# Reordering the start, the output add and the scale loads of a fused retention and mixture-of-experts kernel on one core

## What is computed

```python
# block 1: chunked retention, 8 heads of 16, chunks of 64 tokens
x = x + retention(layernorm(x), Wq, Wk, Wv) @ Wo
#   attn  = (q k^T) * D              inside a chunk, D a decay table
#   o     = attn v + (q * decay_q) S
#   S_new = decay_s * S + (k * decay_k)^T v
# block 2: 8 experts, each token takes the best 2
x = x + ffn(layernorm(x))
#   probs = softmax(n @ Wg);  top 2, weights divided by their sum
#   h = square(relu(n @ W1[e]));  y = h @ W2[e];  out = sum_e combine[e] * y
```

## Time and profile before

| | us |
|---|---|
| three runs | 320.14, 324.41, 324.46 (median 324.41) |
| the profiled execution: its own time | 321.02 |
| its span, first to last instruction | 319.2 |
| PE busy in the span | 285.7 (90%) |
| DVE, POOL, ACT busy | 216.2, 205.5, 180.4 |
| mean granted TensorE clock, of full speed | 0.957 |

### The profile page before, as it was taken

The page is one execution under the profiler, slowest core; times in us unless marked ns, Lnnn a source line. Parts: engine busy times, 40 slices in busy tenths (PEclk is TensorE's granted clock), DMA queues, the critical chain, the costliest instruction groups (busy, mean ns, idle before and its releaser), DMA issues.

```text
span 319.2 us, 8925 instructions
## 1 busy us (share of the span) xinstructions
PE 285.7 (90%) x3662; PEld 224.8 (70%) x3662; DVE 216.2 (68%) x561; ACT 180.4 (57%) x258; POOL 205.5 (64%) x166
## 2 busy tenths in 40 slices
PE   7968838898899889998999879998999889989995
PEld 5655537576688667875888658876888668868883
DVE  2853805788176965599476945599476927998873
ACT  2451633555387465756476545756476545767772
POOL 2134628968366885777985794777985767466553
PEclk9996995799799999999999998999999999999999
DMA  7345009007001261033402180000700070016000
GB/s 244 104 132 169 2 23 310 3 2 239 30 1 35 70 206 61 0 101 104 166 3 65 37 258 10 0 35 24 247 1 36 6 264 1 25 47 227 3 33 33
DMA packets 13577, 26.80 MB, mean 84 GB/s; under 512 B 1120, under 2 KB 6624, under 8 KB 13536
## 3 DMA queue, kind: packets, MB, share of 16 engines
q1 hardware_dynamic: 13536, 26.23, 25.1%
HBM read 24.00 MB, written 2.23 MB: 82 GB/s over the span
## 4 chain that ended last, share of the span: by engine, by line
PE 64%; DVE 16%; issue 12%; POOL 5%; ACT 2%; POOLq 1%; DVEq 0%
PE h_ps L323 8%; PE h_ps L325 7%; PE h_ps L324 7%; PE y_ps L338 6%; PE y_ps L344 5%; PE y_ps L339 5%; POOL act_lo L1061 5%; PE bank L471 3%; PE bank L483 3%; DVE attn L650 3%; PE bank L496 3%; DVE act_s L759 2%; DVE out_sb L780 2%; PE bank L404 2%; DVE combine_r L749 2%
## 5 line engine op out<-in xcount | busy, mean ns | idle before, releaser
L1061 POOL TENSOR_TENSOR act_lo<-act_f,act_hi 128x512 fp32r<-128x512 f32 x112 | 146.8, 1332 | 68.4 <-ACT act_f L946 68.3
L759 DVE SCALAR_TENSOR_TENSOR act_s<-h_ps,scale 128x1024 f32<-128x1024 f32 x64 | 78.1, 1220 | 61.2 <-PE h_ps L325 58.2
L941 ACT ACTIVATE act_hi<-act_s 128x1024 fp32r<-128x1024 f32 x64 | 68.0, 1063 | 58.8 <-DVE act_s L759 58.7
L946 ACT ACTIVATE act_f<-act_s 128x1024 f32<-128x1024 f32 x64 | 66.9, 1046 | 0.0
L323 PE MATMUL h_ps<-x_hi,w_lo 128*128 128x512 f32 x128 | 54.4, 425 | 3.2 <-ACT o_t L912 3.2
L338 PE MATMUL y_ps<-act_hi,w_lo 128*128 128x512 f32 x128 | 54.8, 428 | 2.0 <-issue 2.0
L325 PE MATMUL h_ps<-x_hi,w_hi 128*128 128x512 f32 x128 | 51.7, 404 | 0.0
L324 PE MATMUL h_ps<-x_lo,w_hi 128*128 128x512 f32 x128 | 51.7, 404 | 0.0
L339 PE MATMUL y_ps<-act_hi,w_hi 128*128 128x512 f32 x128 | 51.6, 403 | 0.0
L344 PE MATMUL y_ps<-act_lo,w_hi 128*128 128x512 f32 x128 | 41.2, 403 | 0.1
L323 PEld LDWEIGHTS h_ps<-x_hi,w_lo 128*128 128x128 f32 x128 | 24.9, 195 | 8.8 <-ACT o_t L912 3.4
(11 more groups left out here) (135 smaller groups left out, 413.3 us busy)
## 6 DMA issues: line engine op xcount, KB each, us to landing
scale<-scratch SPq DMA_DIRECT2D x32, 512.0 KB, 6.0
x_t_in<-x_tr SPq DMA_DIRECT2D x8, 256.0 KB, 4.2
x_all<-x SPq DMA_DIRECT2D x8, 256.0 KB, 4.2
out<-out_sb SPq DMA_DIRECT2D x8, 256.0 KB, 2.1
scale<-w SPq DMA_DIRECT2D x1, 768.0 KB, 4.8
cst<-constants SPq DMA_DIRECT2D x1, 417.0 KB, 5.3
cst<-constants SPq DMA_DIRECT2D x1, 256.0 KB, 2.8
scale<-w SPq DMA_DIRECT2D x1, 256.0 KB, 6.1
```

What stands on the lines that cost most here:

```text
L759: nc.vector.scalar_tensor_tensor(out=act_s[:, u % 2], in0=h_ps[:, u % 2], scalar=0.0, in1=scale[:, f % 2, e].unsqueeze(1).to_broadcast([P, ...
L941: nc.scalar.activation(act_hi[:, u % 4], act_s[:, u % 2], ACT.Square).then_inc(act_hi_ready, 1)
L946: nc.scalar.activation(act_f[:, u % 2], act_s[:, u % 2], ACT.Square).then_inc(act_f_ready, 1)
L1061: nc.gpsimd.tensor_tensor(act_lo[:, u % 4, n], act_f[:, u % 2, n], act_hi[:, u % 4, n].bitcast(F32), ALU.subtract).then_inc(pool_low_ready, 1)
```

## The change

Six edits, all of them in the order of work:

- **Start.** On TensorE the products of tile 1 go further forward, the W1 pieces behind them, and `transpose_roots(0)` stands ahead of `w1_product(0, 0)`; ScalarE's and GpSimd's orders follow.
- **Router.** `route` uses `x_sum` and `wg_whole` in float32, 4 products in place of 8, and doesn't wait for `x_lo`. `shift_logits` reads the logits from PSUM without a sum first.
- **`low_x`** goes from GpSimd, ahead of `low(u + 1)`, to VectorE, behind `scale_h(f, 6)`.
- **Small products.** `outputs_within` is cut into halves in slots 13 and 14, `outputs_before` goes from slot 14 to slot 15. `transpose_roots` goes from slot 11 to slot 12.
- **VectorE.** `spread_roots` stands behind the second `decay_scores` product of four, and its sum becomes a `tensor_reduce`. `add_experts(f - 1)` goes from behind `scale_h(f, 3)` to behind `scale_h(f, 7)`.
- **Quarters.** The four quarters of `scale` get waits that spread them in time.

```diff
             def scales(s):
...
                 for j in range(PARTS):
-                    if s >= 2:
-                        sp.wait_ge(act_s_ready, EXPERTS * (s - 2) + PER_PART * (j + 1))
+                    if j == 0 and s >= 2:
+                        sp.wait_ge(act_s_ready, EXPERTS * (s - 1))
+                    if j == 1 and 1 <= s and s + 1 < TILES:
+                        sp.wait_ge(av_done, s + 2)
+                    if j >= 2:
+                        sp.wait_ge(act_s_ready, EXPERTS * s + 2 * j - 3)
...
             def route(s):
-                r = s % X2T_RING
-                pe.wait_ge(x_hi_ready, s + 1)
-                pe.wait_ge(x_lo_ready, s + 1)
                 pe.wait_ge(x_sum_ready, s + 1)
+                pe.wait_ge(x_hi_ready, s + 1)
...
-                for g in range(GROUPS):
-                    o = bank1[:, 2 * EXPERTS * g:2 * EXPERTS * (g + 1)]
-                    pe.matmul(o, x_lo[:, r, P * g:P * (g + 1)], parts, start=True, stop=False)
-                    last = pe.matmul(o, x_hi[:, r, P * g:P * (g + 1)], parts, start=False, stop=True)
+                for g in range(GROUPS):
+                    last = pe.matmul(bank1[:, EXPERTS * g:EXPERTS * (g + 1)], x_sum[:, s % SUM_RING, P * g:P * (g + 1)],
+                                     wg_whole[:], start=True, stop=True)
...
-                    if n == 11:
+                    if n == 12:
                         transpose_roots(p)
...
                     if n == 13:
-                        outputs_within(a)
+                        outputs_within(a, (0, 1))
                     if n == 14:
+                        outputs_within(a, (2, 3))
+                    if n == 15:
                         outputs_before(a)
...
-                nc.vector.tensor_tensor(combine_r[:].rearrange("p e g -> p g e"), spread[:, :, 0], spread[:, :, 1],
-                                        ALU.add).then_inc(combine_ready, 1)
+                nc.vector.tensor_reduce(combine_r[:], spread[:].rearrange("p g k e -> p e g k"), AX_X, ALU.add
+                                        ).then_inc(combine_ready, 1)
...
                 scale_h(f, 3)
                 low(u + 2)
-                if f >= 1:
-                    add_experts(f - 1)
                 if p < TILES:
                     choose(p)
...
                 if a < TILES:
-                    decay_scores(a, decay_order(a)[1:])
+                    decay_scores(a, decay_order(a)[1:2])
                 if p < TILES:
                     spread_roots(p)
+                if a < TILES:
+                    decay_scores(a, decay_order(a)[2:])
                 scale_h(f, 5)
...
                 scale_h(f, 6)
                 low(u + 5)
+                if p < TILES:
+                    low_x(p)
                 if a + 1 < TILES:
                     statistics(a + 1, 0)
                 scale_h(f, 7)
                 low(u + 6)
+                if f >= 1:
+                    add_experts(f - 1)
```

More of the change, by code:

```diff
@@ L460, in state_updates, with outputs_within @@
                 last.then_inc(u_done, 1)
-            def outputs_within(s):
+            def outputs_within(s, groups):
                 b = s % 2
-                pe.wait_ge(attn_ready, PAIRS * (s + 1))
-                pe.wait_ge(update_ready, 2 * (s + 1))
-                for g in range(GROUPS):
+                if groups[0] == 0:
+                    pe.wait_ge(attn_ready, PAIRS * (s + 1))
+                    pe.wait_ge(update_ready, 2 * (s + 1))
+                for g in groups:
                     for j in range(2):
@@ L565, in _ @@
             project_qk(1)
-            outputs_within(0)
+            outputs_within(0, (0, 1, 2, 3))
+            project_v(1)
             outputs_before(0)
+            transpose_k(1)
+            project_out(0)
+            scores(1)
+            transpose_x2(0)
             center_piece(1)
-            project_out(0)
-            project_v(1)
-            transpose_k(1)
-            transpose_x2(0)
-            scores(1)
             route(0)
+            project_qk(2)
             center_piece(2)
-            project_qk(2)
+            transpose_k(2)
             center_piece(3)
-            transpose_k(2)
             center_piece(4)
+            transpose_roots(0)
+            w1_product(0, 0)
+            state_updates(1)
             project_v(2)
-            state_updates(1)
-            w1_product(0, 0)
-            outputs_within(1)
+            outputs_within(1, (0, 1, 2, 3))
             outputs_before(1)
-            transpose_roots(0)
             w1_product(0, 1)
@@ L1088, in _ @@
                     root_variance(p, 1)
-                    low_x(p)
                 low(u + 1)
```

112 lines of the change are left out of this document (51 added, 61 removed).

## The result

The changed kernel takes **330.94 us** in the median of four runs (329.40 to 335.95), the kernel before in the same comparison 323.80 (320.14 to 324.46). The ratio is 1.022, with a 95% interval from 1.013 to 1.031: it is slower, though whether by more than 2% stays open. The forecast was 323, near no change, with a range of 307 to 335: the time lies in the range, but the kernel got slower where no change was forecast. The profiled execution took 329.40, its span 327.6, at a mean granted clock of 0.951.

The account below looks back on a forecast made before the run. The prediction took TensorE, busy for 90% of the span, and its idle gaps as the bound. From the profiled execution: 321.0 - 11 - 7.3 - 7.7 - 3.0 + 26.3 + 5.0 = 323.3 us, forecast 323, range 307 to 335.

Parts of the forecast that it names:

- the start: Ahead of the first W2 product: the new order wins 11 us, between 8 and 13; under 8 refutes the prediction.
- The output add and SyncE's order: Tile boundaries: the store waits for the late add, delaying scratch write and quarters; 26.3 us plus 5.0 of half clock.
- The root wait: At `transpose_roots` in the loop: the wait for `combine_r` goes, a gain of 7.3 of 8.25 us.
- Issue stalls: TensorE's four issue gaps in the loop go because quarters start later: 7.7 us, plus 3.0 for clock dips.
- The third rival: Loop: issue stalls stay since bursts of small products cause them, not the quarters; 334 us, slower, chance 0.12.
- Router and low part: Router time stays 0.9 us; `low_x` gives VectorE 0.97 a turn, counted in the output add's term.
- the second: Boundaries: the scratch write queues behind the loads and the clock falls each time; 337 us, slower, chance 0.17.
- The first rival: Boundaries: short hand-over, scratch 2.85 and 1.8 us, no dips; 306 us, or 309 with less start gain; faster, chance 0.28.

Follow-up runs that it names:

- e1: The changed kernel with the output add moved back behind `scale_h(f, 3)`; 299.98 us, ratio to before 0.926.
- e2: The changed kernel with SyncE issuing the store behind the loads and the next tile's quarters; 298.37 us, ratio to before 0.919.
- e4: The changed kernel with 14 products of zeros added ahead of `transpose_x2` in turns 2 to 6; 330.95 us.
- e7: e2 with the small products unspread, placed as in the kernel before; 300.50 us.
- e8: The changed kernel with both loads behind scratch write and quarters, the store still first; 324.66 us, ratio to before 0.999.
- e9: e2 with the quarters' waits and the small products' places both as in the kernel before; 302.31 us.
- e11: e5 with `transpose_roots` back in slot 11; 301.23 us, ratio to before 0.935.
- e12: e9 with `transpose_roots` back in slot 11; 320.41 us.
- e5: e2 with the first quarter of tile 0 waiting for the end of `outputs_before(1)`; 296.70 us, ratio to before 0.917.
- e13: e5 with the small products spread in turns 0 and 1 only; 297.95 us, ratio to before 0.925.
- e10: e5 with `low_x` back on GpSimd ahead of `low(u + 1)`; 297.07 us, ratio to before 0.921.

## Why the prediction was wrong, and where it was right

- **The step that failed: the start, "… and `copy_o` end at 40.4 … and `w1_product(0, 1)` ends near 42 … so I take 11, between 8 … and 13."** The first W2 product started at 55.29 and not at 49.4, 6.2 earlier than before, and the first pair 6.9 earlier. The prediction had named a start that wins less than 8 as a sign that it is wrong. Its later part held: 7.4 us were counted from the end of `w1_product(0, 1)` to the first W2 product, and from 47.9 to 55.29 it is 7.4. What failed is the part ahead of it, where the end came at 47.9 in place of 42:

```profile
44.45 0.65 ACT L922 COPY o_t<-h_ps 128x256 f32<-128x256 f32 x2 [3.05 <-PE h_ps L480]
...
45.15 0.80 PE L320 MATMUL h_ps<-x_hi,w_lo 128*128 128x512 f32 x1 [0.74 <-ACT o_t L922]
```

  The roots of tile 0 came at 34.79 where 33.3 was worked out, which is 1.5 of the 5.9. `copy_o` ended at 45.1 and not at 40.4: ScalarE stood 3.05 ahead of it, since TensorE had the stall of 3.17 inside the 192 small products of tile 1, under the first two quarters that the earlier roots had brought there. Then TensorE was at half clock from 43 to about 49.6, and the six products took 2.9 in place of 1.6. The sum had no term for a stall there; the low end of 8 counted the stalls of before, and this one was 1.61 then, with idle DMA engines.
- **The range of this term was missed too.** The six profiled kernels with the same code and waits at the start (after, e1, e2, e4, e7, e8) have their first pair at 56.2 to 61.5, 1.6 to 6.9 us earlier than before. Part of that spread can be read: in e4 and e8 the router of tile 0 is already some 2 us later than in after (26.15 and 26.09 against 24.06), and e2, e4, e7 and e8 have a second stretch of about 7 us at half clock, between 31 and 41, which after and e1 don't have. Why kernels with the same code differ in this stays open.
- **The output add and SyncE's order: right in mechanism, place and sum.** VectorE stands 8.5 to 9.2 us in the three turns with loads and 6.2 to 6.4 in the others, where 7 to 9 was forecast. The scratch write starts behind store and loads, and TensorE waits ahead of `transpose_x2`. From the end of the add to the landing of the scratch write it is 5.0, 4.3 and 4.8, for 4.5. The block was put at 26.3 + 5.0 = 31.3, and e2 gives 32.1 in the loop and 32.6 in the medians. Its parts are off in opposite directions: gaps of 21.5 for 26.3, and busy time at half clock of 9.35 for 5.0, of which e4 gives back under half. The rest of the 32, some 7 us, isn't split further here. Half clock came with the four gaps of 3.81 to 4.78 and not with those of 1.75 and 1.99, as forecast.
- **The root wait: right.** No gap is left at `transpose_roots`. The sum of `combine_r` takes 0.27, for 1.18 in the loop before. The new wait of 1.0 that was given back is 2.6: 1.19 and 0.33 for `attn` in turn 0, 1.05 for `x_lo` ahead of the last tile.
- **Issue stalls: the result right, the reason wrong.** They went and the loop's gain is there (e2's loop is 16.8 shorter than before; -7.3 - 7.7 - 3.0 is -18.0). But "Quarters now start behind `outputs_before` …" is not why: e9 has the old waits and the old bursts and keeps 2.6 us of them. The later roots alone are enough for most of it (e9), and so are spreading and pacing together (e11 has none in the loop); with all three away (e12) 14 us are there. Spreading alone and pacing alone, with early roots, were not tried. The third rival had half of it right: bursts make stalls by themselves (e5, e13), and the quarters make them longer.
- **Router and low part at zero: right for the low part** (e10). The router was not tried alone; its eight records take 0.88 to 1.03 us, for 0.9.
- **The sum.** The profiled execution is 6.1 us above the 323.3: 4.1 from the start, 2.0 from the loop (the table of the first section). In the loop the gains are 1.2 smaller (16.8 for 18.0) and the block of the output add 0.8 larger (32.1 for 31.3). So the missed start is the larger part, and that the time still lies in the range is partly owed to the range being wide enough to take in the rivals. The medians differ by 7.1, the two profiled executions by 8.4.
- **Slips that change little.** In the earlier trace rows there are two dips in the loop and not three, and those at the start are slices 4, 7 and 8. By the prediction's own parts the boundary from 5 to 6 comes to 2.65 and not 2.8, and from 6 to 7 to 4.3 and not 4.4.

Of the rivals, the second (337) had the right direction and too high a price; its condition, a scratch write landing over 5.5 us behind the add, was not met, but came near with 5.0, 4.3 and 4.8. The first rival counted on 2.85 and falls. The scratch write landed 2.2, 2.7 and 2.6 us behind its issue where loads were ahead of it, 1.7 where none were (227.45). In each of the three it landed about 0.1 behind `x_t_in`: for the rows above, 110.24 + 2.8 = 113.0 and 110.93 + 2.2 = 113.1. By the Trainium skill, "DMA: Bandwidth & Descriptors", section "Queues, rings and completion order", an increment lands only behind the earlier writes of its DMA engine. By that rule, the trace agrees. The delay alone proves nothing, since the scratch write also took 2.9 at the start of after (35.07) with idle DMA engines and up to 3.2 in before. What kept the price under the rival's is that these loads landed in 2.8 to 3.3 us and not in the 5.1 of the earlier trace rows.

## What to carry to other kernels

Before an instruction is moved to a later place, look at which queue waits for its result and what stands behind that wait; here one store in front of a scratch write turned a free move into 32 us, and moving it behind the write turned a slower kernel into one that is 8% faster than before. When a reorder brings something earlier, ask what its transfers will then lie on: in these kernels bursts of small products under full DMA engines stopped TensorE for 0.9 to 4.65 us. A gap's half clock, read off as busy time times the missing clock, was more than it cost here: of 7.65 us taken away, 3.5 came back.

## What the runs showed of the hardware

- TensorE stalls with no wait in the profile ("issue") during or right behind bursts of 32x64 and 64x64 products. With idle DMA engines it was 1.16 to 1.80 us at the start (e5, e10, e11, e13) and 1.28 in the loop (e13). With full ones it was up to 4.65 at the start and 4.19 in the loop (e12).
- Such a stall often ended near the end of the transfers: 0.75 us behind it (81.35 in before), 0.35 ahead of it (120.45), 1.3 behind (43.62 in after) and 0.6 behind (117.65 in e12). In before at 189.96 and 260.54 the engines stayed full for over 1 us more, and in e9 for 4 us. That TensorE's own instructions come over the same DMA engines is the likely reason and only argued. The page of every kernel lists two DMA queues of the kind "instruction", with some 29 and 12 packets and 0.58 MB together, but not when they ran. By the Trainium skill, "Runtime: NRT & Kernel Launch", section "Instruction fetch mechanics", the cost of a block's crossing is mostly hidden. If these stalls are fetches, they are where it isn't; no run here shows that.
- SyncE itself can be held at an issue: that of the same 256 KB load took 0.43 to 1.68 us on SyncE. That its queue was full then is not shown.
- The same sum of pairs on VectorE, as an addition of two operands, took 1.18 us in the five tiles in which GpSimd was busy with `low` all the while (for the earlier trace rows, from 142.09 to 147.11), and 0.22 in the three in which it began with GpSimd idle (34.61, 70.56 and 282.96 in before). As a reduction of one operand it took 0.27 to 0.28 in all eight, six of them beside the same busy GpSimd. So 0.9 us of the old 1.18 hung on what GpSimd did; the prediction put the whole gain on the form, by a row of another reduction.
